# Moving the routing steps of two units one and a third tiles further back in a four-unit mixture-of-experts kernel

## What is computed

```python
x = x + gated_copy(_ln_c(x))                # gate from two depthwise lines
t = _to_tokens(x)                           # 4096 tokens of 128 channels per image
t = t + moe(_ln_t(t), gate 0, experts 0)    # top 2 of 8 experts, 128 -> 512 -> 128, gelu
x = _from_tokens(t, x)
x = x + pools(_ln_c(x))                     # max pools 1, 3, .. 13, two of them weighted per channel, + x
t = _to_tokens(x)
t = t + moe(_ln_t(t), gate 1, experts 1)
```

## Time and profile before

| what | us |
|---|---|
| median of 3 runs (lowest, highest) | 1134.44 (1126.28, 1143.79) |
| the profiled execution | 1131.95 |
| its span, first to last instruction | 1130.2 |
| TensorE matmul busy | 832.7 (74%) |
| VectorE busy | 566.2 (50%) |
| ScalarE busy | 522.3 (46%) |
| GpSimd busy | 620.7 (55%) |

### The profile page before, as it was taken

One profiled execution on the slowest core, in us unless ns is written; L12 is line 12 of the kernel. 1 busy time (PEld: TensorE's weight loads), 2 busy tenths in 40 slices (PEclk: granted clock), 3 DMA queues, 4 the chain that ended last, 5 costly groups with the idle time before them and its releaser, 6 DMA issues.

```text
span 1130.2 us, 14753 instructions
## 1 busy us (share of the span) xinstructions
PE 832.7 (74%) x4305; PEld 701.0 (62%) x4305; DVE 566.2 (50%) x1308; ACT 522.3 (46%) x1427; POOL 620.7 (55%) x598
## 2 busy tenths in 40 slices
PE   1854389888977777986787579976886877778780
PEld 1434267776776665865777467866776755657680
DVE  8957902280500292999883577999481003300004
ACT  1405045453454445653294256642483534444463
POOL 1000266766766655688634555788545665656651
PEclk9876579988988877998689598987797987879895
DMA  7001343443465752454157633533255645636356
GB/s 315 1 0 65 128 144 116 138 134 111 157 210 187 231 191 89 148 158 131 42 153 249 229 120 110 184 119 97 69 137 195 209 154 163 204 113 213 113 182 223
DMA packets 55391, 167.63 MB, mean 148 GB/s; under 512 B 13888, under 2 KB 13901, under 8 KB 55056
## 3 DMA queue, kind: packets, MB, share of 16 engines
q1 hardware_dynamic: 36880, 130.98, 34.7%
q0 software_dynamic: 18432, 35.70, 11.2%
HBM read 137.26 MB, written 31.46 MB: 149 GB/s over the span
## 4 chain that ended last, share of the span: by engine, by line
PE 43%; DVE 23%; ACT 11%; issue 9%; another core or an unknown queue 9%; DMA 2%; POOL 1%; SPq 0%; POOLq 0%; ACTq 0%; DVEq 0%
PE h_ps L773 15%; PE yT_ps L786 14%; DVE state L1292 5%; PE turn_ps L708 5%; ACT hT L586 4%; DVE work L1278 4%; DVE work L1273 4%; PE acc_ps L725 3%; PE acc_ps L745 2%; DVE work L1286 2%; PE xT_ps L762 2%; ACT yT L597 1%; ACT work L624 1%; PE yr_ps L796 1%
## 5 line engine op out<-in xcount | busy, mean ns | idle before, releaser
L501 POOL DMA_INDIRECT xg<-xn_rows,tile_rows x288 | 307.7, 1068 | 247.1 <-DVEq L1208 126.7
L510 POOL DMA_INDIRECT y_rows<-yr,tile_rows x288 | 308.8, 1072 | 238.6 <-ACT yr L606 157.2
L773 PE MATMUL h_ps<-xT,expert 128*128 128x256 f32 (+1 forms) x1408 | 327.3, 382 | 76.6 <-issue 40.9
L786 PE MATMUL yT_ps<-hT,expert 128*128 128x256 f32 (+1 forms) x1408 | 310.6, 373 | 40.8 <-ACT yT L597 37.3
L586 ACT ACTIVATE hT<-h_ps,expert 128x256 f32<-128x256 f32 (+1 forms) x704 | 254.6, 449 | 153.5 <-PE h_ps L773 62.9
L773 PEld LDWEIGHTS h_ps<-xT,expert 128*128 128x128 f32 x1408 | 250.3, 214 | 116.4 <-issue 75.0
L786 PEld LDWEIGHTS yT_ps<-hT,expert 128*128 128x128 f32 x1408 | 254.6, 212 | 80.6 <-ACT yT L597 45.2
L1242 DVE SCALAR_TENSOR_TENSOR tok<-work,share,tok 128x128 f32<-128x128 f32 x224 | 61.5, 345 | 343.4 <-DMA work<-y_rows 341.4
L597 ACT ACTIVATE yT<-yT_ps,expert 128x256 f32<-128x256 f32 (+1 forms) x176 | 74.1, 443 | 188.0 <-PE yT_ps L786 87.3
L574 ACT ACTIVATE xT<-xT_ps 128x256 f32<-128x256 f32 x144 | 56.4, 392 | 97.5 <-PE xT_ps L762 64.7
L762 PE MATMUL xT_ps<-ident,xg 128*128 128x128 f32 x288 | 61.7, 298 | 40.3 <-DMA xg<-xn_rows,tile_rows 32.8
(11 more groups left out here) (210 smaller groups left out, 644.3 us busy)
## 6 DMA issues: line engine op xcount, KB each, us to landing
expert<-in_experts SPq DMA_DIRECT2D x176, 514.5 KB
work<-y_rows SPq DMA_DIRECT2D x24, 512.0 KB
xn_rows<-work SPq DMA_DIRECT2D x16, 512.0 KB, 5.0
xg<-xn_rows,tile_rows POOLq DMA_INDIRECT x288
y_rows<-yr,tile_rows POOLq DMA_INDIRECT x288
tok<-in_x_tokens SPq DMA_DIRECT2D x8, 512.0 KB, 7.0
state<-in_x SPq DMA_DIRECT2D x2, 2048.0 KB, 17.4
work<-y_rows SPq DMA_DIRECT2D x16, 256.0 KB, 6.0
```

The costliest lines, as they stand in the source:

```text
L501: pool.indirect_dma_start(xg[:, s, h, :], None, xn_rows[unit], bass.IndirectOffsetOnAxis(ap=tile_rows[unit % 2][:, at, 0, h:h + 1], axis=0)) \
L510: pool.indirect_dma_start(y_rows[unit], bass.IndirectOffsetOnAxis(ap=tile_rows[unit % 2][:, at, 1, h:h + 1], axis=0), yr[:, s, h, :], None ...
L773: mm = pe.matmul(h_ps[c // 2][:, c % 2, cols], expert[:, t.load(h) % W_RING, c * P:(c + 1) * P], xT[:, t.slot(2), cols], start=True, stop= ...
L786: mm = pe.matmul(yT_ps[:, cols], expert[:, t.load(h, d) % W_RING, HIDDEN + c * P:HIDDEN + (c + 1) * P], hT[:, s, c, cols], start=(c == 0), ...
```

## The change

Only the two `mixing` entries of `WHEN` are changed.

```diff
-    mixing(0, read=3, state=(6, 7, 7.6, 8), norm=11, route=(28, 28.3), slots=30.3, rows=(30, 31, 31.6, 33),
-           invert=(33, 33.3, 34, 34.3)),
-    mixing(1, read=2, state=(4, 5, 5.6, 6), norm=7, route=(25, 25.6), slots=28, rows=(27.3, 28.6, 29.3, 30),
-           invert=(30.3, 30.6, 31, 31.3)),
+    mixing(0, read=3, state=(6, 7, 7.6, 8), norm=11, route=(29.3, 30), slots=31.3, rows=(31, 31.6, 32.3, 34),
+           invert=(34, 34.3, 35, 35.3)),
+    mixing(1, read=2, state=(4, 5, 5.6, 6), norm=7, route=(26.3, 27), slots=29, rows=(28.6, 29.3, 30, 31),
+           invert=(31.3, 31.6, 32, 32.3)),
```

## The result

The changed kernel takes 1142.3 us (median of 20 runs) against 1138.2 for the kernel before in the same series: a ratio of 1.0055, 95% interval 1.003 to 1.008. The medians are over all runs, the ratio leaves out those in which the chip was in a slower state. By the ratio the kernel is slower by about 6 us where 10.6 less were forecast.

A forecast was written before the change was run, and what follows sets the result against it. The prediction saw TensorE waiting for VectorE's pooled state, gathers pacing the gaps, and boundary waits. Unit 1's boundary 3.7, unit 2's halves 4.9 and the tile's lead 2.0 gave 10.6 us less, 1121.3, as a median 1124; range 1108 to 1141.

The forecast's parts named there:

- The gaps: TensorE's waits of 12.13 us (unit 1) and 7.34 us (unit 2) filled; first half 1.3 us to spare, then 3.6 late.
- The halves: Second half of the turn: unit 1 starts as before at 553.7; unit 2 ends at 798.0, 4.9 us earlier.
- The clock: TensorE after the two waits: filling the gap should keep the upper level, where 0.61 of it was granted before.
- The first rival: TensorE's clock stays up through both halves: 17.6 us gained, 1117 us; chance 0.2.
- Counts and inversion follow with the same lists: Unit 2, after the second half: the last inversion group ends at 844.4, where it ended at 849.33.
- the pause left out: Unit 2, middle of the second half: a pause of 3.35 us not counted in the end at 798.0.
- Unit 1's boundary: Tile 32's scatter moves ahead of the last two groups; GpSimd gathers at 608.2 instead of 611.94, gaining 3.7 us.
- The wait of 2 to 3 us at the counts: Unit 1: TensorE reaches the counts 2 to 3 us earlier and waits that long for `chosen_any`.
- The sum: Whole kernel: -3.7 - 4.9 - 2.0 = -10.6 us, so 1121.3, with the median at 1124.
- the lead of a tile: End of unit 2: one tile more is done than before, worth nothing to 4 us in unit 3; 2.0 taken.
- The queues: Unit 2: SP's four stores stand behind two more weight loads but keep their place relative to the rows, at no cost.
- The slower rival: Unit 2's gather pace makes the second half end at 809.3, 6.4 us later; net 2.7, 1137 us; chance 0.1.

The follow-up runs named there:

- before_paced: Kernel before, its own order, with GpSimd filling an unused tile (1.2 us) once per step at steps 27 to 31 of unit 1 and 22 to 28 of unit 2: 0.9943.
- pace_block: Changed kernel with GpSimd filling an unused tile (1.2 us) once per step at steps 27 to 31 of unit 1 and 22 to 28 of unit 2: 0.9814.
- u1_only: Kernel before with only unit 1's entry changed, unit 2's as before: 0.9967 of the kernel before.
- inv_early_u2: Changed kernel with unit 2's inversion put back at its places in the kernel before: 1.0026 of the kernel before.
- hold_pool: Changed kernel with GpSimd waiting once in each of units 1 and 2 until the block's last product is made: 1.0035 of the kernel before.
- pace_half: Changed kernel with GpSimd filling half of an unused tile (0.69 us) per step, at steps 27 to 31 of unit 1 and 22 to 28 of unit 2: 0.9984.

## Why the prediction was wrong

*The gaps* came out as worked. Unit 1: a wait of 2.92 ahead of the first half (1.3 was forecast), gather waits of 1.83 and 2.23. Unit 2: gather waits of 2.04 and 2.56, no wait for the state, and the first half at 787.01 where 783.9 plus the offset gives 788.6.

*The halves* too. The second half of unit 2's turn was to end at 798.0; it ended at 799.2, or 794.5 without the offset, so the 4.9 us were won and more. *The clock* was above the 0.61 of the earlier trace rows: 0.89 from 787 to 804, most of the way at the upper level, and 0.50, the lower one, in the trickle. The first rival's condition was thus met in unit 2, and its time of 1117 wasn't. The Trainium skill's rule (TensorE: Matmul & The Clock Gate, "HAM oscillation") that idle gaps put the clock back agrees with the 0.89, ahead of which no long wait stood. That transposes don't count ("Part 4: PE-mode transpose") isn't tested by these rows: eight of them took 1.04 us and the products behind them 3.64, but other matmuls stood on both sides.

*The step that failed* is "Counts and inversion follow with the same lists". Two terms were missing behind it, and both lie on the way from the second half to the rows:

1. "with ... the pause left out": the pause of 3.35 us that no engine of the profile explained reads now as the start of the stall, cut short because GpSimd came to wait for ScalarE. For it: with the same order and GpSimd paced (before_paced) no such pause stands there. That GpSimd's wait ended it is argued from the times alone. The new order takes that wait away and the stall runs on. From second half to choice it cost 5.9 us more in unit 2 (26.9 against 21.0) and some 6 in unit 1 (23.5 against 17.5).
2. The same list between counts and inversion is walked by an engine that is now a tile further on in its other work: TensorE was 6.3 us late for one-hots that were ready. The prediction carried the early second half through to the last group, as though VectorE alone set it. With the stall gone this term takes back what unit 2 gained: in pace_block the choice is 3.6 us earlier than in before_paced, the first group 4.9 us late.

In unit 2, from the end of the state: second half 4.7 earlier, second half to choice 5.9 longer, choice to one-hots 3.9 shorter (the old order's execution had a stall of its own at the counts), late inversion 6.2 longer, the groups 0.5 shorter: the last group comes 3.0 later, where 4.9 earlier was forecast.

*Unit 1's boundary* went as told in its order: the scatter out of the way, the gather at once. Its 3.7 us don't show while the stall is there: in the change and in u1_only the late rows ate them, and image 1's state ends as far behind image 0's as before. With GpSimd paced unit 1 brings more, 12.5 us. The wait of 2 to 3 us at the counts was missing in the change and is there, 2.61, once GpSimd is paced: the forecast was of a kernel without the stall.

*The sum* on paced kernels, 14.7 us for the 10.6 of the forecast, is near it by luck: by the traces unit 1 brings 12.5 where 3.7 was said, and unit 2 up to the gather for unit 3 nothing where 4.9 was. The 2.0 for *the lead of a tile* is shown by no run: from that gather to the end the executions take 271.3 to 280.6 us (sixteen, in which nothing behind it was edited), in either order.

*The queues* were put at no cost. That held only because the rows were late as well; inv_early_u2 shows the stores as the last condition of GpSimd's wait.

*The slower rival* had the sign but not the mechanism: it decided from a second half ending after 806.6, and it ended at 799.2. Both the range and the rivals lacked a case in which removing a wait on one engine lets another run on into its neighbour.

## What to carry to other kernels

A pause "that the profile doesn't explain" is a cost with a cause: before leaving it out of a sum, look at which engine starts or stops issuing at both its ends. A wait that a change removes may have throttled someone else, so follow the engine that no longer waits, not only the one that gained. And price the consumer at the end of the chain: an earlier half is worth something only if the matmuls that use it, and the stores beside them, stand early enough in their queues.

## What the runs showed of the hardware

While GpSimd issued indirect transfers back to back every 1.3 us, TensorE's instructions fell to one every 0.7 to 1.4 us, 8 to 13 us after GpSimd had reached that rate (the change, hold_pool, pace_half), and its signals were late too (a product of 804.1 reached VectorE at 816.72), with the DMA share at 0.18; 1.2 us of other work on GpSimd in every 6.4 took the effect away. The rate alone doesn't always bring it: in unit 3 of the changed kernel GpSimd issued so from 982.8 to 998.1, and none of TensorE's instructions has "issue" ahead of it there. What else is needed isn't shown. During the pooling GpSimd's issues took 32.09 / 26 = 1.23 us each and later 134.91 / 137 = 0.98, so it is the end of the pooling that sets the full rate free.

The Trainium skill (SBUF — State Buffer, "SBUF: two separate sides") says that VectorE in some modes locks GpSimd out of a shared port, which would fit the slower issues, though no run here shows the mode, and that TensorE's port waits for no one. The second doesn't explain this case: TensorE did ten matmuls in 12 us while GpSimd ran free. Whether it stopped at that port, which path the two share, and whether the loading of instructions has a part, isn't shown by any run here.
